# Twelve of 208 edge groups move from the count-matrix path to the row-gather path in a four-layer graph network

## The reference

```python
# layer 0: an edge network and a mean over the edges of each node, then a node network
h = relu(concat(x[row], edge_attr) @ W1a + b1a) @ W1b + b1b
agg = segment_sum(h, col) / max(cnt, 1)
z = relu(concat(x, agg, u[batch]) @ W2a + b2a) @ W2b + b2b
# layer 1: degree-scaled sum over the edges, a residual, batch norm
agg = segment_sum((x * rsqrt(deg_out))[src], dst) * rsqrt(deg_in)
y = relu(agg @ W + b) + relu(x @ Wr + br)
# layer 2: mean over the edges
z = elu((segment_sum(x[src], dst) / max(deg, 1)) @ W + b)
# layer 3: twice, four relations with weighted edges
m = sum_r [type == r] * (x[src] @ W_r) * ew ;  h = segment_sum(m, dst) + x @ root + b
```

## Time and profile before

| | us |
|---|---|
| median of 3 timed runs | 3857.17 |
| lowest and highest | 3850.79, 3857.61 |
| span of the profiled execution | 4761.8 |
| engines busy in it: PE, DVE, ACT, POOL | 3833.3, 2287.6, 2017.5, 2652.2 |
| mean granted clock of PE, share of full speed | 0.874 |
| gathers in it | 2707 of the 2744 POOL instructions |
| pass 0, 1, 2, then 3 and 4 (first gather or wide product to last instruction of the pass) | 1344.8, 364.6, 383.8, 2415.6 |

### The profile page before, as it was taken

One profiled execution on the slowest core, in us unless ns is written; L12 is line 12 of the kernel. 1 busy time (PEld: TensorE's weight loads), 2 busy tenths in 40 slices (PEclk: granted clock), 3 DMA queues, 4 the chain that ended last, 5 costly groups with the idle time before them and its releaser, 6 DMA issues.

```text
span 4761.8 us, 69331 instructions
## 1 busy us (share of the span) xinstructions
PE 3833.3 (81%) x23096; PEld 3228.5 (68%) x23096; DVE 2287.6 (48%) x7830; ACT 2017.5 (42%) x4824; POOL 2652.2 (56%) x2744
## 2 busy tenths in 40 slices
PE   5888888888888997899577778777766777777777
PEld 4777777777776886788466666555555666766666
DVE  5777777777676555666434334333321222222222
ACT  3444434444445554565444444444443333433332
POOL 5666666566542654555565565555656556564554
PEclk7999998998899998999788888888887788888878
DMA  6555555555555664666234333333333334443333
GB/s 197 151 147 149 152 149 150 148 148 149 144 151 145 149 152 105 160 172 165 89 127 137 128 134 131 125 116 127 127 114 105 118 113 124 128 125 112 121 115 97
DMA packets 438618, 642.39 MB, mean 135 GB/s; under 512 B 266274, under 2 KB 310818, under 8 KB 438115
## 3 DMA queue, kind: packets, MB, share of 16 engines
q1 hardware_dynamic: 310162, 375.66, 25.2%
q0 software_dynamic: 100880, 235.32, 18.7%
q10 hardware_dynamic: 27202, 26.78, 1.8%
HBM read 468.80 MB, written 168.73 MB: 134 GB/s over the span
## 4 chain that ended last, share of the span: by engine, by line
PE 28%; another core or an unknown queue 10%; issue 8%; DVE 5%; ACT 1%; DVEq 0%; DMA 0%; POOL 0%; ACTq 0%; POOLq 0%; SPq 0%
PE bank L1715 9%; PE bank L1654 6%; PE bank L1679 4%; PE bank L1700 3%; PE bank L1690 3%; PE bank L1645 1%; DVE w_both L1489 1%; DVE work L1557 1%; DVE work L1489 1%; DVE late_lo L1537 1%; PE bank L2353 0%; PE bank L2370 0%; DVE work L1582 0%; ACT work L2665 0%
## 5 line engine op out<-in xcount | busy, mean ns | idle before, releaser
L652 POOL DMA_INDIRECT work<-table_rel,reli x1462 | 1385.7, 948 | 1060.0 <-issue 426.4
L652 POOL DMA_INDIRECT work<-table_pre,srci x831 | 816.7, 983 | 537.6 <-issue 237.3
L2660 ACT ACTIVATE work<-iota,local 128x72 f32<-128x72 f32 x1464 | 378.4, 344 | 609.1 <-remote 346.8
L1034 ACT ACTIVATE X<-bank 128x468 uint8<-128x468 f32 (+1 forms) x624 | 323.9, 545 | 708.7 <-PE bank L976 375.1
L1654 PE MATMUL bank<-work 128*128 128x72 f32 x2928 | 425.0, 290 | 245.9 <-issue 234.8
L1654 PEld LDWEIGHTS bank<-work 128*128 128x128 f32 x2928 | 417.4, 212 | 265.5 <-issue 242.5
L2665 ACT ACTIVATE work<-work,ew,src_both 128x72 f32<-128x72 f32 x1464 | 515.4, 436 | 15.7 <-remote 9.7
L937 PE MATMUL bank<-w_both,work 128*128 128x256 f32 x1664 | 473.2, 409 | 33.3 <-issue 14.5
L1406 PE MATMUL bank<-counts,piece_hi 128*128 128x468 f32 x1176 | 464.7, 395 | 28.4 <-issue 12.9
L1406 PE MATMUL bank<-counts,piece_lo 128*128 128x468 f32 x1176 | 450.2, 383 | 0.0
L949 PE MATMUL bank<-work 128*128 128x64 f32 x3328 | 423.0, 281 | 22.3 <-issue 21.4
(11 more groups left out here) (326 smaller groups left out, 6489.9 us busy)
## 6 DMA issues: line engine op xcount, KB each, us to landing
work<-ea_cols SPq DMA_DIRECT2D x208, 256.0 KB
kept<-work SPq DMA_DIRECT2D x50, 880.0 KB
kept<-w_both SPq DMA_DIRECT2D x50, 880.0 KB
work<-kept SPq DMA_DIRECT2D x50, 880.0 KB
w_both<-kept SPq DMA_DIRECT2D x50, 880.0 KB
adj<-X SPq DMA_DIRECT2D x156, 225.0 KB
work<-adj SPq DMA_DIRECT2D x60, 585.0 KB
work<-table_rel,reli POOLq DMA_INDIRECT x1462
```

The lines of the kernel that those rows point to most:

```text
L652: pool.indirect_dma_start(into[:, u, :], None, tables[p], bass.IndirectOffsetOnAxis(ap=idx_of(p)[:, t:t + 1].bitcast(U32), axis=0)).then_i ...
L1034: act.activation(stage[:, j % A_STAGES, lo * AW:hi * AW], bank[A_BANKS_AT[b % 2]][:, 0:(hi - lo) * AW], ACT.Copy).then_inc(a_taken, 1)
L2660: ins = act.activation(hot3[:, u, :], iota[:, 0:PAIR_WIN], ACT.Abs, bias=local[:, t:t + 1], scale=-1.0)
```

## The change

One place of each body after the first, the last near one of its first half (place 5: `LEFT_OUT`), goes from near to far. 144 near groups are left, 64 are far. A step has D = 12 groups and a product 12 x 36 = 432 columns; the number of steps and of products stays. `FAR_AT` gives each step 4, 5 or 6 far groups, and `PARTS_AT` has a row for 6. In pass 0 the 12 groups lose codes, fill, takes and store; all counters of these go by the number of near groups instead of by body and place. The base numbers are sorted by eight copies per pass instead of two. Passes 3 and 4 wait for the new totals and are otherwise the same.

```diff
@@ -38,14 +38,16 @@
 DENSE = [q for q in range(BODY) if q % SLOTS < NEAR]
 SPARSE = [q for q in range(BODY) if q not in DENSE]
 D0 = len(DENSE)
-NEAR_GROUPS = [g for g in range(GROUPS) if g % BODY in DENSE]
-FAR_GROUPS = [g for g in range(GROUPS) if g % BODY not in DENSE]
+LEFT_OUT = DENSE[NEAR - 1]
+NEAR_GROUPS = [g for g in range(GROUPS) if g % BODY in DENSE and (g < BODY or g % BODY != LEFT_OUT)]
+FAR_GROUPS = [g for g in range(GROUPS) if g not in NEAR_GROUPS]
+NEARS = len(NEAR_GROUPS)
 FARS = len(FAR_GROUPS)
 HOPS = 12
 TURNS = HOPS + 1
 D = len(NEAR_GROUPS) // HOPS
 S = 4
-FAR_AT = (0, 5, 10, 14, 18, 22, 26, 31, 35, 39, 44, 48, FARS)
+FAR_AT = (0, 6, 12, 17, 22, 28, 33, 38, 44, 49, 54, 60, FARS)
 AW = 36
 A_OFF = (0, 2, 10, 18)
 A_WIDE = (12, 18, 18, 18)
...
 PARTS, LOADS, A_SLOTS, ON_ACT = CHUNKS, CHUNKS // 2, 4, 7
-PARTS_AT = {4: ((0, 1, 2), (3, 4), (5, 6, 7), (8, 9)), 5: ((0, 1), (2, 3), (4, 5), (6, 7), (8, 9))}
+PARTS_AT = {4: ((0, 1, 2), (3, 4), (5, 6, 7), (8, 9)), 5: ((0, 1), (2, 3), (4, 5), (6, 7), (8, 9)),
+            6: ((0, 1), (2, 3), (4, 5), (6, 7), (8,), (9,))}
...
 
-        def codes(dve, g, d, j):
+        def codes(dve, g, d):
             dve.wait_ge(a_filled, d * 4 + 4)
             for u in range(U):
-                ins = dve.tensor_scalar(code[:, j % A_CODES, A_AT[u]:A_AT[u + 1]],
+                ins = dve.tensor_scalar(code[:, d % A_CODES, A_AT[u]:A_AT[u + 1]],
                                         iota_h[:, A_OFF[u]:A_OFF[u] + NT * A_WIDE[u]], codef[:, bass.ds(g * U + u, 1)], None,
                                         ALU.is_equal)
             ins.then_inc(code_ready, 1)
...
-                    if (q - HOTS) % BODY in DENSE:
-                        d = DENSE.index((q - HOTS) % BODY) - (0 if q >= HOTS else D0)
-                        dve.wait_ge(a_filled, it * D0 * 4 + (d + 1 + A_CODES) * 4)
+                    if n + q - HOTS in NEAR_GROUPS:
+                        dve.wait_ge(a_filled, (NEAR_GROUPS.index(n + q - HOTS) + 1 + A_CODES) * 4)
                     one_hot(dve, n + q, n + q, q)
                     if it or q >= LAG:
                         accumulate(dve, at[q], n, q, LAG - q)
-                    if q in DENSE:
-                        codes(dve, n + q, it * D0 + DENSE.index(q), DENSE.index(q))
+                    if n + q in NEAR_GROUPS:
+                        codes(dve, n + q, NEAR_GROUPS.index(n + q))
...
         LAST_AGGS = [AGG_AT[g] for g in AGG_AT if g >= GROUPS]
-        FILLED_AT = {k: (g // BODY * D0 + sum(q < g % BODY for q in DENSE)) for g, k in AGG_AT.items()}
+        FILLED_AT = {k: sum(near < g for near in NEAR_GROUPS) for g, k in AGG_AT.items()}
...
 
-            def fill(d, q, b):
-
-                j = DENSE.index(q)
+            def fill(g, q, b):
+                d = NEAR_GROUPS.index(g)
                 lo, hi = A_BANKS[b]
                 if b == 0:
-                    pe.wait_ge(code_ready, d + j + 1)
-                pe.wait_ge(a_taken, (d + j) * 4 + b + 1)
-                if b == 0 and q % SLOTS == 0 and d // D0 * BODY + q - 1 in AGG_AT:
-                    pe.wait_ge(n0_kept, 2 + AGG_AT[d // D0 * BODY + q - 1])
+                    pe.wait_ge(code_ready, d + 1)
+                pe.wait_ge(a_taken, d * 4 + b + 1)
+                if b == 0 and q % SLOTS == 0 and g - 1 in AGG_AT:
+                    pe.wait_ge(n0_kept, 2 + AGG_AT[g - 1])
...
                     mm = pe.matmul(into[:, :, A_OFF[u]:A_OFF[u] + w], hot_lo[q % HOTS][:, u, :],
-                                   code[:, j % A_CODES, at:at + (hi - lo) * w].rearrange("p (h w) -> p h w", w=w),
+                                   code[:, d % A_CODES, at:at + (hi - lo) * w].rearrange("p (h w) -> p h w", w=w),
...
@@ -989,23 +990,23 @@
             def body(it):
                 n = it * BODY
                 for q in range(BODY):
-                    dense = q - 1 in DENSE
+                    dense = n + q - 1 in NEAR_GROUPS and q > 0
                     more_pre = n + q + LAG < GROUPS
                     if dense:
-                        fill(it * D0, q - 1, 0)
+                        fill(n + q - 1, q - 1, 0)
...
 
             def take(it, q, b):
-                j = DENSE.index(q)
-                d = it * D0 + j
+                d = NEAR_GROUPS.index(it * BODY + q)
                 lo, hi = A_BANKS[b]
                 if b == 0:
-                    act.wait_ge(a_stored[j % A_STAGES], (it * (D0 // 2) + j // 2) * 16 + 16)
+                    act.wait_ge(a_stored[d % A_STAGES], d // A_STAGES * 16 + 16)
                 act.wait_ge(a_filled, d * 4 + (b + 1 + 4 * A_CODES))
-                act.activation(stage[:, j % A_STAGES, lo * AW:hi * AW], bank[A_BANKS_AT[b % 2]][:, 0:(hi - lo) * AW], ACT.Copy
+                act.activation(stage[:, d % A_STAGES, lo * AW:hi * AW], bank[A_BANKS_AT[b % 2]][:, 0:(hi - lo) * AW], ACT.Copy
                                ).then_inc(a_taken, 1)
...
 
             def store(d):
-                j = d % D0
                 sp.wait_ge(a_taken, d * 4 + 6)
                 sp.sem_inc(gate, 1)
-                sp.dma_start(adj[d:d + 1, :, :].rearrange("o p c -> p (o c)"), stage[:, j % A_STAGES, :]
-                             ).then_inc(a_stored[j % A_STAGES], 16)
+                sp.dma_start(adj[d:d + 1, :, :].rearrange("o p c -> p (o c)"), stage[:, d % A_STAGES, :]
+                             ).then_inc(a_stored[d % A_STAGES], 16)
...
                     load(g // BODY * BODY, g, g % BODY, pre_done, ea_ready)
-                if g >= A_LAG and (g - A_LAG) % BODY in DENSE:
-                    store((g - A_LAG) // BODY * D0 + DENSE.index((g - A_LAG) % BODY))
+                if g - A_LAG in NEAR_GROUPS:
+                    store(NEAR_GROUPS.index(g - A_LAG))
...
 
+        def runs(places):
+            starts = [q for q in places if q - 1 not in places]
+            return [(lo, next(q for q in range(lo, BODY + 1) if q not in places)) for lo in starts]
...
             far = (p - 1) * FARS
-            done(dve, dve.tensor_copy(wide_base[:, 0:GROUPS - FARS].rearrange("o (t q) -> o t q", q=NEAR),
-                                      basei[:, LAG:LAG + GROUPS].rearrange("o (t q) -> o t q", q=SLOTS)[:, :, 0:NEAR]))
-            done(dve, dve.tensor_copy(wide_base[:, GROUPS - FARS:].rearrange("o (t q) -> o t q", q=SLOTS - NEAR),
-                                      basei[:, LAG:LAG + GROUPS].rearrange("o (t q) -> o t q", q=SLOTS)[:, :, NEAR:]))
+            bases = basei[:, LAG:LAG + GROUPS]
+            for to, groups in ((0, NEAR_GROUPS), (NEARS, FAR_GROUPS)):
+                first = sum(g < BODY for g in groups)
+                for lo, hi in runs([g for g in groups if g < BODY]):
+                    at = to + groups.index(lo)
+                    done(dve, dve.tensor_copy(wide_base[:, at:at + hi - lo], bases[:, lo:hi]))
+                every = len([g for g in groups if BODY <= g < 2 * BODY])
+                rest = wide_base[:, to + first:to + len(groups)].rearrange("o (t q) -> o t q", q=every)
+                later_bases = bases[:, BODY:].rearrange("o (t q) -> o t q", q=BODY)
+                for lo, hi in runs([g - BODY for g in groups if BODY <= g < 2 * BODY]):
+                    at = groups.index(lo + BODY) - first
+                    done(dve, dve.tensor_copy(rest[:, :, at:at + hi - lo], later_bases[:, :, lo:hi]))
 
             def load_near(it, lo, hi):
                 return load_wide(dve, it * D + lo, hi - lo)
 
             def load_far(it):
-                return load_wide(dve, GROUPS - FARS + FAR_AT[it], fars(it))
+                return load_wide(dve, NEARS + FAR_AT[it], fars(it))
...
```

More of the change, by code:

```diff
@@ L998, in body @@
                     if dense:
-                        fill(it * D0, q - 1, 1)
+                        fill(n + q - 1, q - 1, 1)
                     segment_sum(n + q, q)
@@ L1003, in body @@
                     if dense:
-                        fill(it * D0, q - 1, 2)
+                        fill(n + q - 1, q - 1, 2)
                     if more_pre:
@@ L1007, in body @@
                     if dense:
-                        fill(it * D0, q - 1, 3)
+                        fill(n + q - 1, q - 1, 3)
             with pe.If(before > 0):
@@ L1050, in pass0_act @@
                 for q in range(BODY):
-                    if q - 2 in DENSE:
+                    if q >= 2 and it * BODY + q - 2 in NEAR_GROUPS:
                         take(it, q - 2, 0)
@@ L1504, in gnn @@
         CODES_BEFORE, FILLS_BEFORE, TAKES_BEFORE, USES_BEFORE = (
-            ITERS0 * D0, (A_CODES + ITERS0 * D0) * 4, 2 + ITERS0 * D0 * 4, 2 * HOPS * PARTS)
-        KEPT_BEFORE = ITERS0 * (D0 // A_STAGES) * 16 + 16
+            NEARS, (A_CODES + NEARS) * 4, 2 + NEARS * 4, 2 * HOPS * PARTS)
+        KEPT_BEFORE = NEARS // A_STAGES * 16 + 16
         def built_setup(dve, of, tmp, first, lo, code_of, w):
@@ L1766, in node0_sp @@
             for s in a_stored:
-                sp.wait_ge(s, ITERS0 * (D0 // A_STAGES) * 16 + 16)
```

(3 more changed lines are left out.)

## The result

The changed kernel takes 3870.04 us (median of 4 runs, 3869.35 to 3877.86), the kernel before 3855.36 beside it; the ratio is 1.0043, 95% interval 1.0032 to 1.0055. The change makes the kernel slower by 0.4%, where 0.65% faster (3832 us) was forecast.

A forecast was written before the change was run, and what follows sets the result against it. PE, the fullest engine, was taken to bound passes 0, 1 and 2. The terms -17.0 - 36.5 + 21.6 + 2.8 + 4 = -25.1 us took 3857.2 to 3832 us, with a range of 3806 to 3868.

The forecast's parts named there:

- PE is the bound of a steady step: Passes 1 and 2: PE is busy for 26.87 of a 27.0 us step and 29.00 of a 29.0 us one.
- Part 3: Passes 1 and 2: 24 more gathered groups add 0.90 us each on PE, 21.6 us; their gathers stay hidden behind PE.
- the 4 us for late gathers: Pass 1: added because gathers lie near the point where PE no longer covers them; half of that pass's 7.4 us gain.
- Part 1: Pass 0: 12 groups lose their fill, 1.42 us of PE work each, 17.0 us off; bounds nothing and 34 us.
- Part 2: Passes 1 and 2: 2352 products of 432 columns in place of 468 save 0.0155 us each, 36.5 us off.
- rival 2: Passes 1 and 2: the weight load sets the spacing of wide products, so fewer columns bring nothing; 3865 us, chance 0.06.
- Rival 1: Gathers become the bound from 1.24 us each: pass 1 +11, pass 2 -2, pass 0 nothing; 3869 us, chance 0.14.
- Rival 4: Pass 0 gives its upper bound, 34 us, as a group's turn falls from 6.54 to 4.40 us; 3811 us, chance 0.12.
- Rival 3: A tie: pass 0 gives nothing, gathers just pace pass 1, pass 2 gives 7.4 us; 3853 us, chance 0.18.
- the spacing of 0.196 us: Sign for being right: wide products of passes 1 and 2 spaced at about 0.196 us, against 0.21 before.
- the step of 26.4 us: Sign for being right: a steady step of pass 1 of some 26.4 us, PE full and gathers waiting for slots.
- the gather pace above 1.24 us: Sign for being wrong: gathers in the timed run take 1.24 us or more each; the estimate was 1.1.

## Why the prediction was wrong

| | forecast, us | in the undisturbed records |
|---|---|---|
| pass 0, fills | -17.0 | -5.4, within the spread of the same code |
| 2352 products | -36.5 | 2352 x 0.015 = -35 |
| 24 far groups, own products | +21.6 | 24 x 0.81 = +19.4 |
| 24 far groups, all that they cost | +25.6 (with the 4 below) | +55 to +59, by the run without them |
| copies of base numbers | +2.8 | not seen: last gather of pass 0 to first wide product 94.8 to 94.1 |
| gathers late in pass 1 | +4 | segment sums wait 6 in passes 1 and 2 |
| PE waits for DVE at node parts | none | +9.2 and +12.8 |

- **What bounds the kernel.** The first reading, PE as the bound of pass 0, failed. So did "PE is the bound of a steady step": it was read off, and both stretches there are steps with 4 far groups. The text called them steps with 4 or 5.
- **The step that failed: Part 3**, which priced a far group by its products alone and held its gathers to be covered. With the 4 us for late gathers that made 25.6 us; the run without the 24 groups prices them at 55 to 59. For the products 0.90 was nearly right (1.006 - 0.197 = 0.81: from the last wide product before to the first after, less one spacing). Two costs were missing:
  - *PE's wait for DVE.* A far group also moves a step from one row of `PARTS_AT` to another, and that row decides how many products stand ahead of a node part. By the products the two parts together give -35 + 19.4 = -15.6 us for passes 1 and 2; they came out at +18.7. Of the difference PE spent 22 us more in these two waits and 6 us more waiting for gathers. About 6 us stay open; the mean granted clock does not explain them, for it is 0.94 and 0.96 in both records.
  - *The gathers of pass 1.* The 22 us say where PE stood, not what each wait is worth. In pass 2 the row change gives back 28.4 us, so there DVE's wait is the cause. In pass 1 it gives back only 4.1, because the gathers end the pass next: with the rows changed in both kernels pass 1 is still 16.9 us longer after the change. In pass 1 the two causes hide each other, and its loss of 7.0 us belongs to neither alone.
- **It could have been seen.** The old record's steps of pass 2 with 4 groups and with 5 stood side by side:

```profile
2097.20:2126.90 29.70, 29.39 (x152) 24.64 (x151) 19.25 (x54) 18.69 (x20) 14.98 (x16) 1.00 0.65 170
2127.00:2161.40 34.40, 31.95 (x160) 27.00 (x158) 19.93 (x56) 18.59 (x20) 21.07 (x22) 0.95 0.60 159
```

- **Part 1** failed where it took PE's work for the time of pass 0. Its own lower bound, nothing, because the gathers pace the pass, was the answer. It was set aside because PE was the fullest engine, and in Part 3 by "I hold the timed pace to be below that". The prediction had counted 3841 us for a run in which gathers hardly wait, saw that only 16 us were left, and took the count as a sign of faster gathers. For the gathers the count was right as it stood: they run at 1.25 us at the median in every record, and in the undisturbed ones they hardly wait in passes 0, 3 and 4. What it left out is that in each of passes 1 and 2 four steps have 5 groups and take longer than the 27.0 and 29.0 us it gave to all twelve.
- **Part 2** was right, rival 2 wrong. By the Trainium skill (TensorE: Matmul & The Clock Gate, section Back-to-back issue gap) loads and products set the spacing together; here it followed the columns, 0.212 to 0.197 us, and the load did not hold it up.
- **Rival 1** named 3869 us, and 3870 was measured; that the numbers agree is chance. It had +11 us for pass 1 and -2 for pass 2; measured were +7.0 and +11.7. Its condition was met ((252.6 + 75.3) / 255 = 1.29 us per gather in pass 1, above 1.24), but the step it was weighed against never got as short as 26.4 us: PE waited for DVE first. Segment sums waited 2.9 us for gathers in pass 1, gathers still 10.1 for slots. Where the row change takes DVE's wait away, rival 1 appears as it was worked out: +16.9 us in pass 1 and -2.3 in pass 2 between the two kernels with their rows changed.
- **Rival 4** fell with pass 0. **Rival 3** was right on pass 0, which gave nothing that stands clear of its spread, but where it had 7.4 us of gain in pass 2, the pass lost 11.7.
- **The signs.** Of those for being right, the spacing of 0.196 us came; gathers still waited for slots, but less (10.1 us in pass 1 against 62.5 before); the step of 26.4 us did not come. Of those for being wrong, the gather pace above 1.24 us came.

## What to carry to other kernels

Before an item is priced by its own instructions, compare two neighbouring steps that differ by just that item: the difference holds what a price list leaves out, here 2.9 to 5.4 us against 0.8. (It is an upper price: over all 24 groups the mean was 2.3 to 2.5 us, and not every added group moved a step to another row.) After one wait is found, ask what ends last without it: here taking DVE's wait away gave pass 2 back 28 us and pass 1 only 4. Where the order of work is written out by hand in rows by count, a change of the count is a change of the row, and each product that waits for another engine should be checked for how much work stands ahead of it (here 0.26 us of margin decided). And where a count that gives a stage to one engine's own pace comes out within half a per cent of the timed run, as here for the gathers, that is a reason to hold that engine for the stage's bound; a record much longer than the timed run is to be taken again before its waits are believed.

## What the runs showed of the hardware

A gather of 128 rows starts 1.25 us (median) after the one before when nothing holds it up, in every record, the disturbed one included: 0.944 to 0.947 us busy and 0.305 of pause that no instruction fills, so that the pause belongs to its price. A stretch of disturbed record can mimic another bound: the same kernel had 1060.0 us of idle time ahead of the gathers of passes 3 and 4 in one record and 493.8 in another. PE's clock can be part of the price of a wait. In the kernel before, the four steps of pass 1 with 5 groups had 5.0 us less busy time, for the same instructions, once they no longer waited at the node product. But a wait does not always cost clock: in pass 1 of the changed kernel two steps with 6 groups both wait 1.6 us, one at a mean clock of 0.94 with 28.57 us of busy time, the other (shown above) at 1.00 with 27.06.

```profile
1349.20:1379.40 30.20, 28.57 (x161) 27.10 (x160) 15.37 (x41) 14.80 (x17) 20.11 (x22) 0.94 0.56 146
```
